# The layers' opening of a two-branch attention kernel: VectorE forms the rotary cosine products, and the first tile is rotated ahead of the second's sums

## The reference, cut to what matters

```python
q, k, v = jnp.split(h @ wqkv, 3, axis=-1)          # 8 heads of 64 each
q = l2norm(q) * qs
k = l2norm(k) * ksc
# rotary_xpos
q = q * cos * scale + rotate_half(q) * sin * scale
k = k * cos / scale + rotate_half(k) * sin / scale
o = local_attention(q, k, v)
```

## Time and profile before

| | |
|---|---|
| median of 3 runs | 1930.73 us (1926.85 to 1933.4) |
| the profiled execution | 1927.33 us, its span 1925.2 us |
| busy: TensorE, VectorE, ScalarE, GpSimd | 1823.5, 1231.2, 1374.2, 881.4 us |
| TensorE's share of the chain that ended last | 75% |
| the layers' opening, first projection to first scores | 658.92 to 699.62 us |
| mean granted clock of TensorE | 0.984 |

### The profile page before, as it was taken

The page is one execution under the profiler, slowest core; times in us unless marked ns, Lnnn a source line. Parts: engine busy times, 40 slices in busy tenths (PEclk is TensorE's granted clock), DMA queues, the critical chain, the costliest instruction groups (busy, mean ns, idle before and its releaser), DMA issues.

```text
span 1925.2 us, 47714 instructions
## 1 busy us (share of the span) xinstructions
PE 1823.5 (95%) x17808; PEld 1565.2 (81%) x17808; DVE 1231.2 (64%) x4126; ACT 1374.2 (71%) x3998; POOL 881.4 (46%) x1302
## 2 busy tenths in 40 slices
PE   6999999999999879999999999999999999999998
PEld 4788788788778658888898897888888888889787
DVE  5543544445443357777777777787777777777765
ACT  5886978788688556857758668677576685775864
POOL 3533543344243455536436355364473553654631
PEclk9999999999999979999999999999999999999999
DMA  4321321322223620111101101314112112010110
GB/s 148 101 77 44 113 87 54 91 96 88 74 91 99 210 69 23 48 42 32 51 26 45 57 15 53 107 33 163 45 40 64 34 48 65 23 59 26 43 48 29
DMA packets 125018, 128.11 MB, mean 67 GB/s; under 512 B 26632, under 2 KB 100082, under 8 KB 124788
## 3 DMA queue, kind: packets, MB, share of 16 engines
q1 hardware_dynamic: 121620, 118.77, 19.9%
q10 hardware_dynamic: 3168, 6.29, 1.0%
HBM read 72.44 MB, written 36.85 MB: 57 GB/s over the span
## 4 chain that ended last, share of the span: by engine, by line
PE 75%; ACT 10%; DVE 6%; POOL 3%; DMA 2%; SPq 2%; issue 1%; DVEq 0%; POOLq 0%; ACTq 0%
PE f_bank L1454 18%; PE a_bank L630 16%; PE f_bank L1593 10%; PE f_scores L1608 5%; PE f_o_bank L1568 5%; PE a_o_bank L727 4%; PE f_scores L1535 4%; ACT f_prob L1677 3%; PE f_bank L1546 3%; PE a_bank L712 2%; PE a_scores L704 2%; PE f_bank L1507 2%; POOL a_prob L610 2%; PE f_bank L1550 1%; DVE f_u L1817 1%
## 5 line engine op out<-in xcount | busy, mean ns | idle before, releaser
L1418 POOL TENSOR_SCALAR f_prob<-f_prob,f_row_inv 128x192 f32<-128x192 f32 x512 | 224.4, 457 | 391.9 <-DVE f_row_inv L1759 391.9
L610 POOL TENSOR_SCALAR a_prob<-a_prob,a_row_inv,a_gate 128x128 f32<-128x128 f32 x512 | 226.3, 459 | 377.5 <-DVE a_row_inv L948 377.5
L1454 PE MATMUL f_bank<-weights,f_actT 128*128 128x512 f32 x1152 | 300.8, 407 | 1.6 <-DVE f_actT L1710 1.6
L1593 PE MATMUL f_bank<-f_hT,f_w 128*128 128x256 f32 x2112 | 269.1, 283 | 1.1 <-DVE f_gu L1813 1.1
L1593 PEld LDWEIGHTS f_bank<-f_hT,f_w 128*128 128x128 f32 x2112 | 258.5, 188 | 4.1 <-DVE f_gu L1813 2.7
L1454 PEld LDWEIGHTS f_bank<-weights,f_actT 128*128 128x128 f32 x1152 | 210.8, 191 | 46.9 <-DVE f_actT L1710 1.8
L1677 ACT ACTIVATE f_prob<-f_scores,f_neg_max 128x192 f32<-128x192 f32 x512 | 208.0, 427 | 17.7 <-DVE f_neg_max L1751 16.4
L1406 POOL TENSOR_TENSOR f_qk_tok<-f_qk_tok,tables 128x512 f32<-128x512 f32 x128 | 164.5, 1305 | 116.3 <-DVE f_sin_part L1727 116.3
L1697 ACT ACTIVATE f_u<-f_gu 128x256 fp32r<-128x256 f32 x192 | 80.2, 418 | 174.1 <-DVE f_gu L1813 174.1
L1400 POOL TENSOR_TENSOR f_norm<-f_norm,f_minus_half 128x16 f32<-128x16 f32 x64 | 187.7, 2933 | 32.2 <-DVE f_norm L1719 31.4
L838 ACT ACTIVATE a_prob<-a_scores,a_neg_max 128x128 f32<-128x128 f32 x512 | 179.4, 391 | 24.1 <-DVE a_neg_max L939 24.0
(11 more groups left out here) (143 smaller groups left out, 3958.6 us busy)
## 6 DMA issues: line engine op xcount, KB each, us to landing
split_weights<-a_hi_lo SPq DMA_DIRECT2D x16, 512.0 KB, 3.0
x_next<-states SPq DMA_DIRECT2D x32, 256.0 KB, 3.2
tables<-scaled_tables SPq DMA_DIRECT2D x16, 512.0 KB, 5.9
f_x<-states SPq DMA_DIRECT2D x16, 512.0 KB, 5.1
split_weights<-a_hi_lo SPq DMA_DIRECT2D x12, 682.0 KB, 4.7
weights<-split_weights ACTq DMA_DIRECT2D x6, 1024.0 KB, 9.5
f_w<-split_weights SPq DMA_DIRECT2D x4, 1280.0 KB, 10.7
f_v_crossed<-f_v SPq DMA_DIRECT2D x40, 128.0 KB, 2.4
```

Source lines behind the costliest of these rows:

```text
L610: last = nc.gpsimd.tensor_scalar(part, part, row_inv[:, a % 2, head, t:t + 1], gate[:, half, t, h:h + 1], ALU.mult, ALU.mult)
L1418: last = nc.gpsimd.tensor_scalar(part, part, row_inv[:, a % 2, head, t:t + 1], 1.0, ALU.mult, ALU.mult)
L1454: last = nc.tensor.matmul(out, lhs(c, a), rhs(c, b), start=(i == 0), stop=(i == len(order) - 1))
L1593: mm = nc.tensor.matmul(out[:, which * PART:(which + 1) * PART], w1[:, wp, c, col:col + P], hT[:, hp, c, columns_of(a // FH)], start=(i == ...
```

## The change

In the opening GpSimd no longer multiplies by the cosine table. VectorE does it behind its two sines, queries and keys in one instruction, once it has seen that the sines are done; its addition then waits on a semaphore of its own (`opening_cos`). The loop's passes keep the product on GpSimd. The list `before` is changed too: tile 0's rotation (`rope`) now stands ahead of `project_qk` of tile 1, its `rope_sum` ahead of `project_qk` of tile 2, and `rope_sum` of tile 1 ahead of `project_qk` of tile 3.

```diff
--- before.py
+++ after.py
@@ -1102,8 +1102,8 @@
             return kind == "load_x" or kind in F_PREPARE and (a >= (HALVES - 1) * PER_CHUNK[kind] or kind == "load_wqkv")
 
         e, t0 = HALVES - 1, (HALVES - 1) * TILES
-        before = [("load_x", 0), ("load_tables", e), ("transpose_x", e), ("load_x", e), ("project_qk", t0), ("project_qk", t0 + 1),
-                  ("rope", t0), ("project_qk", t0 + 2), ("rope_sum", t0), ("rope", t0 + 1), ("project_qk", t0 + 3), ("rope_sum", t0 + 1),
+        before = [("load_x", 0), ("load_tables", e), ("transpose_x", e), ("load_x", e), ("project_qk", t0), ("rope", t0),
+                  ("project_qk", t0 + 1), ("rope_sum", t0), ("project_qk", t0 + 2), ("rope", t0 + 1), ("rope_sum", t0 + 1), ("project_qk", t0 + 3),
                   ("rope", t0 + 2), ("transpose_qk", t0), ("project_v", t0), ("project_v", t0 + 1), ("project_v", t0 + 2), ("project_v", t0 + 3),
                   ("cross_values", e), ("rope_sum", t0 + 2), ("rope", t0 + 3), ("transpose_qk", t0 + 1), ("rope_sum", t0 + 3), ("transpose_qk", t0 + 2),
                   ("transpose_qk", t0 + 3)]
@@ -1166,7 +1166,8 @@
         clamped = count("clamped", {"project_qk": 1})
         norm_ready = count("norm_ready", {"project_qk": 1})
         sin_ready = count("sin_ready", {"rope": 1})
-        cos_ready = count("cos_ready", {"rope": 1})
+        cos_ready = count("cos_ready", {"rope": 1}, steps=[step for step in program if step[0] is not None])
+        opening_cos = count("opening_cos", {"rope": 1}, steps=[step for step in program if step[0] is None])
         rope_added = count("rope_added", {"rope_sum": 1})
         roped = count("roped", {"rope_sum": 1})
 
@@ -1419,7 +1420,7 @@
                         last.then_inc(normalized.sem, 1)
                 elif kind == "project_qk":
                     norms(it, a)
-                elif kind == "rope":
+                elif kind == "rope" and it is not None:
                     rope(it, a)
                 elif kind == "ln_stats":
 
@@ -1726,11 +1727,16 @@
                 nc.vector.tensor_tensor(by_head(sin_part[:])[:, :, :, lower], raw[:, :, :, upper], sin[:, :, :, lower], ALU.mult)
                 nc.vector.tensor_tensor(by_head(sin_part[:])[:, :, :, upper], raw[:, :, :, lower], sin[:, :, :, upper],
                                         ALU.mult).then_inc(sin_ready.sem, 1)
+                if it is None:
+
+                    dve.wait_ge(sin_ready.sem, sin_ready.past(it, ("rope", a)))
+                    nc.vector.tensor_tensor(raw, raw, table(COS, a % TILES), ALU.mult).then_inc(opening_cos.sem, 1)
 
             def rope_sum(it, a):
 
                 place = qk_tok[:, a % TILES]
-                dve.wait_ge(cos_ready.sem, cos_ready.past(it, ("rope", a)))
+                cosines = opening_cos if it is None else cos_ready
+                dve.wait_ge(cosines.sem, cosines.past(it, ("rope", a)))
                 nc.vector.tensor_tensor(place, place, sin_part[:], ALU.add).then_inc(rope_added.sem, 1)
                 dve.wait_ge(norm_ready.sem, norm_ready.past(it, ("project_qk", a)))
                 dve.wait_ge(rope_added.sem, rope_added.past(it, ("rope_sum", a)))
```

## The result

The changed kernel takes 1919.97 us (median of four runs, 1918.23 to 1921.81); the kernel before, with one run more beside it, 1929.76 (1926.85 to 1933.4). The ratio is 0.9948, 95% interval 0.9929 to 0.9968: faster, by 0.32 to 0.71%. Forecast were 1922.7 us, between 1919.0 and 1927.8, and a gain of 8.0 us; measured are 9.8 us between the medians and 6.9 us between the two profiled spans. The four runs of before lie high: later runs of it, made beside the experiments, have medians of 1927.52 (23 runs) and 1928.13 us (9 runs), and from these the changed kernel is 7.6 and 8.2 us away.

A forecast was written before the change was run, and what follows sets the result against it. The opening was taken as bound by a chain alternating between VectorE and GpSimd while TensorE waits. Scores 6.3 us earlier plus 1.7 us from the first pass gave 8.0 us, so a median of 1922.7 us, range 1919.0 to 1927.8.

The forecast's parts named there:

- VectorE's row, 25.0 us: Opening: four rotations and three tiles' sums back to back on VectorE, ending at 691.35, 5.5 us earlier.
- The powers are hidden: Opening, GpSimd: each power is ready before its scaling wants it, by 2 us at least.
- What comes late on TensorE: Opening: later sums delay key projections and tile 0's second transposes; value projections start at 681.1 instead of 680.33.
- The cover: Opening: TensorE's transposes of tiles 1 and 2 end at 691.1, 0.3 us before VectorE's last scaling.
- Behind the last scaling, 1.9 us: Opening's end: last scaling to first scores takes 1.9 us instead of 2.74; scores at 693.3, 6.3 us earlier.
- The first chunk, 1.7 us: First pass behind the opening: starting with the clock up, it gets 1.7 us shorter.
- both terms: Scores 6.3 us earlier plus 1.7 us from the first pass: 8.0 us gained, between 7.6 and 8.4.
- The clock came along: Rival: TensorE meets last transposes or first scores at 0.50, or later passes lose the gain; gain 5.5 us; chance 0.17.
- TensorE was not the bound: Rival, opening: value projections stay at low clock, scores at 698.7, gain 0.9 us; chance 0.10.
- The cosine product cost 1.23, not 2.52 us: Rival, opening: a VectorE cosine product costs GpSimd's 2.52 us, scores only 1.1 us early; chance 0.05.
- The hold-up: Rival, opening: VectorE's two-input instructions stand still beside GpSimd's powers, scores 5.7 us late, 1936.4 us; chance 0.06.
- The price of a fall, 0.83 us: Start of a pass: a fall of TensorE's clock costs 7.95 - 7.12 = 0.83 us.

The follow-up runs named there:

- filled starts: Changed kernel plus 12 unused identity transposes on TensorE ahead of the third scores of each of the 16 chunks: 1912.17 us, ratio to before 0.9918.
- kept clock: Kernel before plus 40 unused identity transposes on TensorE ahead of the last tile's transposes in the opening: 1926.37 us, ratio 0.9994.
- shared products: Changed kernel with the added identity transposes at chunk starts, and the opening's cosine products of tiles 1 and 3 back on GpSimd: 1914.92 us, ratio to before 0.9923.
- cosine alone: Changed kernel with the opening's old order, cosine products still on VectorE: 1924.39 us, ratio to before 0.9977.
- order alone: Kernel before with only the opening's new order, cosine products still on GpSimd: 1932.37 us, ratio to before 1.0021.
- more powers: Changed kernel with three more powers on GpSimd in the opening, on values that nothing reads: 1918.82 us in a single run.

## Why the prediction was right

*VectorE's row, 25.0 us.* From the first sine (666.39) to the last scaling's end 24.44 us. The cosine product takes 1.22 to 1.23 us as taken from the addition; a tile's rotation takes 5.08 us (680.60 to 685.68, start to start) where it was put at 5.11, and a tile's sums with the clamp 1.39 (679.21 to 680.60) where they were put at 1.53: in the row that gave 1.45 the second sum had to wait for ScalarE's square, which ended at 671.18. The last scaling ended 6.05 us earlier, not 5.5. Most of this is won ahead of the first scaling: it starts 5.29 us behind the clamp (671.60), where it started 10.20 us behind it (676.48), because tile 0's products had stood behind two powers in GpSimd's queue. From there to the fourth scaling 17.99 us pass in place of 19.16.

*The powers are hidden.* GpSimd's powers, and beside them one of VectorE's additions:

```profile
670.27 1.22 DVE L1740 TENSOR_TENSOR f_qk_tok<-f_qk_tok,f_sin_part 128x1024 f32<-128x1024 f32 x1
...
670.44 7.13 POOL L1401 TENSOR_TENSOR f_norm<-f_norm,f_minus_half 128x16 f32<-128x16 f32 x2 [0.59 <-DVE f_norm L1720]
680.77 3.27 POOL L1401 TENSOR_TENSOR f_norm<-f_norm,f_minus_half 128x16 f32<-128x16 f32 x1 [3.20 <-DVE f_norm L1720]
```

The second and third power end at 677.57, a short wait between them included; tile 2's scaling wants the third at 684.54. No scaling waited. Tile 0's scaling (671.60) lies inside the second power and takes 1.23 us. The powers themselves are longer than the 2.9 to 3.0 us forecast: 3.21 us for the first, two in 7.13, and 3.27.

*What comes late on TensorE.* Its timeline, with the idle time ahead of each in brackets:

```profile
669.61 3.04 PE L1455 MATMUL f_bank<-weights,f_actT 128*128 128x512 f32 x12 [1.00 <-DVE f_norm L1716]
...
679.95 0.66 PE L1508 MATMUL f_bank<-ident,f_qk_tok 128*128 128x128 f32 x4 [4.39 <-DVE f_norm L1716]
680.63 7.37 PE L1455 MATMUL f_bank<-weights,f_actT 128*128 128x512 f32 x24
687.84 2.01 PE L1508 MATMUL f_bank<-ident,f_qk_tok 128*128 128x128 f32 x16
```

Tile 2's key projection waits for its bank until 669.61 (669.6 forecast), the second half of tile 0's transposes until 679.95 (680.3), with 4.39 us idle ahead of it; the value projections start at 680.63 (681.1), take 7.37 us, and the transposes of tiles 1 and 2 end at 689.85, 1 us ahead of VectorE's last scaling. The cover that I had put at 0.3 us was there, and wider.

*Behind the last scaling, 1.9 us.* 690.83 to 692.75, 1.92 us, at a clock of 1.00. With the row above, the scores are 6.87 us earlier in place of 6.3.

*The first chunk, 1.7 us.* Measured 1.28 (78.33 to 77.05). The clock was up at its start, but fell in it, at 698. Without that fall the same chunk takes 76.33 us (filled starts, 693.16 to 769.49), or 76.36 with the kept clock. So the low clock at its start had cost 2.0 us, and the new fall took 0.7 of them back. That 1.7 comes so near is in part luck. It was read as what the first pass takes over the second, but the second is the second half of a sequence and has more work (last section); and a fall in the first chunk was not in the sum.

The sum of both terms is 8.15 us at the second chunk, for 8.0 forecast: the scores came 0.6 us earlier than forecast and the chunk gave 0.4 less, which nearly cancel. Later chunks give some of it back in this profile: from the second chunk to the end it is 1.2 us longer than before (8.15 against 6.9 us in the spans). Eight of these 15 chunks begin with a fall of the clock in either profile, but not the same ones. Whether that is chance was not tried; the runs of the changed kernel alone scatter by more (1918.23 to 1921.81).

*The rivals.* The clock came along as far as the first scores. TensorE was not the bound. The cosine product cost 1.23, not 2.52 us. The hold-up did not come, since what is left on GpSimd beside VectorE are powers; with products left there it does come, as the shared products showed.

*What was read wrongly.* The passes of the text are chunks, 16 halves of a sequence, not whole sequences. The price of a fall, 0.83 us, was read from a second half without and a first half with one, over the first 9 us only; over a chunk it is 0.70 to 0.74 us, or about twice that. The 1.70 us of the first pass over the second compared the same unlike halves.

## What to carry to other kernels

Where a chain goes back and forth between two engines, add up the chain and not the engines' load: 1.23 us more of work a tile on VectorE took away 2.5 us on GpSimd and two hand-overs. With the order left as it was, the scalings came 5.48 us apart (from 676.18 to 692.61 in the kernel with the cosine alone) in place of 6.39. Ask too what stands ahead in the other engine's queue: here two powers stood ahead of the first product. An order is tuned to the engine that does the work; the same new order cost 4.1 us with the products on GpSimd and gained 1.2 us with them on VectorE. Where TensorE waits about 2 us at a place that comes back in every chunk, look at the granted clock behind it: filling the wait with work that nobody needs took 7.8 us off 15 chunks and made the fastest kernel here, at 0.9918 of before.

## What the runs showed of the hardware that was not expected

GpSimd's powers and products behave differently beside VectorE, and it matters which begins first. In the kernel with the cosine alone, VectorE's addition of tile 0 and the power of tile 2 on GpSimd (timelines):

```profile
674.85 1.22 DVE L1740 TENSOR_TENSOR f_qk_tok<-f_qk_tok,f_sin_part 128x1024 f32<-128x1024 f32 x1
...
675.02 3.81 POOL L1401 TENSOR_TENSOR f_norm<-f_norm,f_minus_half 128x16 f32<-128x16 f32 x1 [0.60 <-DVE f_norm L1720]
```

And in the changed kernel a sine product of tile 2, beside which tile 3's power begins at 680.77 and takes 3.27 us (above):

```profile
680.60 0.69 DVE L1727 TENSOR_TENSOR f_sin_part<-f_qk_tok,tables 128x512 f32<-128x512 f32 x1
```

A power takes 2.89 to 2.91 us where it begins just ahead of VectorE's next addition (675.08 in the earlier trace rows, 673.80 with the order alone, 669.95 with more powers). Where it begins while one runs, it is longer by most of what is left of that one: by 0.9 us with 1.05 us of the addition left (ending at 676.07), by 0.4 with 0.5 us of the sine left. VectorE's instructions that begin inside a power are not longer at all. GpSimd's cosine products of 128x512 do stretch VectorE's instructions, by 0.8 to 1.1 us each, and are stretched themselves, as the shared products showed. The Trainium skill, "SBUF — State Buffer", section "Who interferes with whom", has a VectorE instruction with two inputs in SBUF contend with a GpSimd instruction that reads SBUF, over ports that it calls an exclusive lock; that whoever issues first has them for its whole length it says of VectorE's 2-port modes, and the prediction took it for this pair too. So read, the rule agrees with these rows for GpSimd's products and for a power that comes second. It disagrees for a power that comes first, which leaves VectorE free for the 2.9 us that it lasts. Why was not tried.

One more difference is not the hardware's. The first and the second half of a sequence differ by 0.7 us at the same clock (76.00 and 76.69 us with the starts filled), just the lower price of a fall. The cause is work. The line that multiplies probabilities by values leaves out the tile ahead of a sequence's first (`if half or tile`), and so has 32 matmuls fewer in a first half. That line alone on TensorE, in a first and a second half with the starts filled (us, busy us, count, clock, DMA share, GB/s):

```profile
846.20:922.20 76.00, 7.79 (x128) 1.00 0.15 43
922.20:998.89 76.69, 8.72 (x160) 1.00 0.13 38
```

It is busy 0.93 us longer in the second half. The two halves that the prediction compared are not the same work.
